# Five extra matmuls per recurrence step, and one PSUM bank for the pre-activation instead of two

## The reference, cut to what matters

```
def step(carry, tgt):
    s, c, alpha = carry
    f = lax.conv_general_dilated(alpha, conv_w, (1,), 'SAME', dimension_numbers=('NCH', 'OIH', 'NCH'))
    e = jnp.einsum('a,bta->bt', va, jnp.tanh(enc_proj + (s @ Wa_s.T)[:, None, :] + jnp.einsum('bft,af->bta', f, Wa_f) + ba))
    e = jnp.where(mask, e, jnp.float32(-1e+30))
    alpha_new = jax.nn.softmax(e, axis=1)[:, None, :]
    g = jnp.einsum('bt,btd->bd', alpha_new[:, 0], hbatch)
    y = jnp.tanh(g @ L_gy_w.T + L_gy_b + s @ L_sy.T) @ L_yy_w.T + L_yy_b
    rec = tgt @ L_ys.T + s @ L_ss.T + g @ L_gs_w.T + L_gs_b
    ig, fg, cg, og = jnp.split(rec, 4, axis=1)
    c_next = _sig(fg) * c + _sig(ig) * jnp.tanh(cg)
    s_next = _sig(og) * jnp.tanh(c_next)
    return ((s_next, c_next, alpha_new), y)
```

## Time and profile before

| what | before |
|---|---|
| median of 3 runs (lowest to highest) | 1775.03 us (1773.21 to 1776.44) |
| span of the profiled execution | 1777.0 us |
| instructions | 43152 |
| TensorE busy | 1506.0 us (85%) |
| VectorE busy | 919.2 us (52%) |
| ScalarE busy | 528.9 us (30%) |
| GpSimd busy | 387.5 us (22%) |
| granted TensorE clock, mean | 0.633 |

### The profile page before, as it was taken

One profiled execution on the slowest core, in us unless ns is written; L12 is line 12 of the kernel. 1 busy time (PEld: TensorE's weight loads), 2 busy tenths in 40 slices (PEclk: granted clock), 3 DMA queues, 4 the chain that ended last, 5 costly groups with the idle time before them and its releaser, 6 DMA issues.

```text
span 1777.0 us, 43152 instructions
## 1 busy us (share of the span) xinstructions
PE 1506.0 (85%) x15683; PEld 1022.2 (58%) x15683; DVE 919.2 (52%) x4293; ACT 528.9 (30%) x2023; POOL 387.5 (22%) x1030
## 2 busy tenths in 40 slices
PE   6547999999888888888888888888888888887999
PEld 3334454544666666666666666666666666664443
DVE  4996643331555555555555555555555555553422
ACT  1342231221333333333333333333333333331211
POOL 3344321220000222222222222222222222222211
PEclk7658999999555555555555555555555555555999
DMA  8330000001200000000000000000000000000000
GB/s 326 141 115 11 1 1 0 1 1 52 77 0 0 0 0 0 0 0 0 0 0 0 0 0 0 0 0 0 0 0 0 0 0 0 0 0 1 1 24 25
DMA packets 17363, 34.51 MB, mean 19 GB/s; under 512 B 7476, under 2 KB 8675, under 8 KB 17332
## 3 DMA queue, kind: packets, MB, share of 16 engines
q1 hardware_dynamic: 17332, 34.10, 5.3%
HBM read 32.00 MB, written 2.10 MB: 19 GB/s over the span
## 4 chain that ended last, share of the span: by engine, by line
PE 62%; DVE 25%; issue 6%; ACT 5%; POOL 1%; DVEq 1%; SPq 1%; DMA 0%; POOLq 0%; ACTq 0%
PE bank L1243 18%; PE bank L1073 11%; PE bank L1193 6%; PE bank L1088 6%; PE bank L1221 5%; ACT eh L960 4%; DVE interT L746 4%; PE bank L1199 4%; DVE krep L764 3%; PE bank L1213 3%; DVE rinv L755 3%; DVE rs L743 2%; DVE g L760 2%; PE bank L1231 2%; DVE gat L771 2%
## 5 line engine op out<-in xcount | busy, mean ns | idle before, releaser
L1243 PE MATMUL bank<-krep,uh 128*128 128x128 f32 x1024 | 313.1, 461 | 23.6
L1243 PEld LDWEIGHTS bank<-krep,uh 128*128 128x128 f32 x1024 | 237.4, 320 | 92.4 <-DVE krep L764 92.4
L493 POOL TENSOR_TENSOR sscale<-ex,rinv 128x8 f32 x256 | 51.3, 200 | 667.6 <-DVE rinv L755 667.6
L1221 PE MATMUL bank<-eh,krep 128*128 128x4 f16 x2048 | 95.3, 168 | 92.5 <-ACT eh L960 92.5
L764 DVE TENSOR_TENSOR krep<-inv,ahn 128x128 f32<-128x128 f32 x512 | 162.2, 356 | 0.0
L1073 PE MATMUL bank<-xT,wbig 128*128 128x512 f16 x672 | 157.2, 386 | 3.7 <-DVE xT L591 3.7
L743 DVE TENSOR_TENSOR rs<-bank,rin 128x8 f32<-128x8 f32 x256 | 42.8, 167 | 198.1 <-PE bank L1199 198.1
L1221 PEld LDWEIGHTS bank<-eh,krep 128*128 128x128 f16 x2048 | 74.1, 105 | 114.0 <-ACT eh L960 114.0
L963 ACT ACTIVATE xs<-gat 64x8 f32<-64x8 f32 x256 | 53.4, 208 | 288.7 <-DVE gat L771 288.7
L955 ACT ACTIVATE interT<-bank 128x128 f16<-128x128 f32 x256 | 71.2, 278 | 216.9 <-PE bank L1193 216.9
L1181 PE MATMUL bank<-enc,identb 128*128 128x128 bf16 x771 | 128.4, 303 | 0.0
(11 more groups left out here) (201 smaller groups left out, 3044.5 us busy)
## 6 DMA issues: line engine op xcount, KB each, us to landing
wbig<-d_gate_qT SPq DMA_DIRECT2D x4, 896.0 KB, 10.1
wbig<-d_up_qT SPq DMA_DIRECT2D x4, 896.0 KB, 20.7
wbig<-d_down_qT SPq DMA_DIRECT2D x1, 3584.0 KB, 30.5
d_out<-x_sb SPq DMA_DIRECT2D x8, 256.0 KB, 2.0
sscale<-d_gate_sT SPq DMA_DIRECT2D x2, 896.0 KB, 8.6
interT<-d_gate_sT SPq DMA_DIRECT2D x2, 896.0 KB, 14.9
sscale<-d_up_sT SPq DMA_DIRECT2D x2, 896.0 KB, 4.2
interT<-d_up_sT SPq DMA_DIRECT2D x2, 896.0 KB, 4.3
```

The source lines that it names most:

```text
L1221: ins = mm(bank[4][:, 4 * gp:4 * gp + 4], hg2[:, j, h, gp * P:(gp + 1) * P], e[:, 4 * h:4 * h + 4], start=(first and gp == 0 and j == 0 an ...
L1243: mm(bank[1 - par][:, 0:P], uh[:, h, :], qv[:, h, :, :], start=False, stop=False, skip_group_check=True)
```

## The change

The pre-activation of every step stands in `bank[0]`, for TensorE and for ScalarE. `bank[1]`, which is free with that, takes the results of a new helper `keep_busy(n)`: one matmul of `n` columns with the bfloat16 identity as the stationary operand and constants of the recurrence (`hg2`, float16, 128 rows) as the moving one. Nothing reads `bank[1]`. It waits for nothing but its turn on TensorE and releases nothing. There are five such calls in a step:

```
                def keep_busy(n):
                    mm(bank[1][:, 0:n], identb[:], hg2[:, 0].rearrange("p h g -> p (h g)")[:, 0:n], start=True, stop=True)
...
                    last.then_inc(s["sp_done"], 1)

+                    keep_busy(256)
                     pe.wait_ge(s["th_s"], l + 1)
...
                    for j in range(2):
                        mm(bank[3][:, 0:8], th_hi, vae2[:, j, :], start=False, stop=False, skip_group_check=True)
+                    keep_busy(256)
                    pe.wait_ge(s["th_lo_ready"], l + 1)
                    mm(bank[3][:, 0:8], th_lo, vae2[:, 0, :], start=False, stop=True, skip_group_check=True).then_inc(s["et_done"], 1)

+                    keep_busy(256)
                    pe.wait_ge(s["eh_ready"], l + 1)
...
                    masks()
-                    context_part(1 - par)
+                    context_part()
+                    keep_busy(256)

                    for h in range(2):
                        pe.wait_ge(s[f"q{h}_ready"], l + 1)
-                        mm(bank[1 - par][:, 0:P], uh[:, h, :], qv[:, h, :, :], start=False, stop=False, skip_group_check=True)
+                        mm(bank[0][:, 0:P], uh[:, h, :], qv[:, h, :, :], start=False, stop=False, skip_group_check=True)
+                    keep_busy(512)
```

More of the change, by code:

```diff
@@ L954, in _ @@
                     act.wait_ge(s["pre_done"], l + 1)
-                    nc.scalar.activation(th_hi, bank[par][:, 0:P], ACT.Tanh).then_inc(s["th_s"], 1)
-                    nc.scalar.activation(th, bank[par][:, 0:P], ACT.Tanh).then_inc(s["th_full"], 1)
+                    nc.scalar.activation(th_hi, bank[0][:, 0:P], ACT.Tanh).then_inc(s["th_s"], 1)
+                    nc.scalar.activation(th, bank[0][:, 0:P], ACT.Tanh).then_inc(s["th_full"], 1)
                     act.wait_ge(s["et_done"], l + 1)
@@ L1176, in masks, with context_part @@
                 mm(bank[3][:, 0:8], etl[:], etr[:], start=True, stop=False, skip_group_check=True)
-            def context_part(par):
+            def context_part():
                 for j in range(3):
-                    mm(bank[par][:, 0:P], identb[:], enc3[:, j, :], start=(j == 0), stop=False, skip_group_check=True)
+                    mm(bank[0][:, 0:P], identb[:], enc3[:, j, :], start=(j == 0), stop=False, skip_group_check=True)
+            def keep_busy(n):
+                mm(bank[1][:, 0:n], identb[:], hg2[:, 0].rearrange("p h g -> p (h g)")[:, 0:n], start=True, stop=True)
             masks()
-            context_part(0)
+            context_part()
             with pe.Fori(0, S // 2) as i:
@@ L1192, in _ @@
                         pe.wait_ge(s["sl_ready" if st is sl else "sh_ready"], l + 1)
-                        last = mm(bank[par][:, 0:P], was2[:, j, :], st[:].unsqueeze(2).broadcast_to([J, B, TH]),
+                        last = mm(bank[0][:, 0:P], was2[:, j, :], st[:].unsqueeze(2).broadcast_to([J, B, TH]),
                                   start=False, stop=(st is sl), skip_group_check=True)
```

## The result

| | before | after |
|---|---|---|
| median | 1774.78 us (1773.21 to 1776.44, 4 runs) | 1911.6 us (1907.34 to 1918.32, 4 runs) |
| ratio to before | | 1.0768, 95% interval 1.0736 to 1.0799 |
| span of the profiled execution | 1777.0 us | 1909.3 us |
| granted clock, mean | 0.633 | 0.628 |
| TensorE busy | 1506.0 us (85%) | 1776.4 us (93%) |

The change makes the kernel **136.8 us slower**. The forecast was 1845 us, 70 slower, with 1744 to 1865 as the range: the direction is right, the size is half of what came.

What follows compares the result with a forecast made beforehand. A chain that goes round each step of 4.52 us at the low clock, not an engine, was taken as the bound. 256 x 0.32 = +82, cut to +70 for occasional high clock: 1775 + 70 = 1845 us, range 1744 to 1865.

Steps and rivals of the forecast that it cites:

- What bounds the kernel now ... L1243 is not late: Ahead of L1193: its other supplier `sl` comes at the same moment, so a twice as fast L1243 would gain nothing.
- The call of 512 ... 0.32 us late: Between L1243 and L1193, low clock: the call makes L1193's matmul on `sl` and the chain behind it 0.32 us late.
- a hole in TensorE's columns of only 0.14 us: Between L1243's last columns (1001.76) and L1193 (1001.90): idle column time that hides part of the call of 512.
- Four calls of 256 ... Cost nothing, at either clock: Ahead of L1206, L1213, L1221 and L1243: each call's 0.21 us fits in its hole of 0.29, 0.26, 0.56 or 0.27.
- I expect that the clock rises now and then, for about one step in nine: In the 256 steps: the high clock in one of nine cuts +82 us, for all steps at the low clock, to +70.
- The direction: Whole kernel: slower than before, given a chance of 0.75.
- seem to count for little: The clock's rule: matmuls of half the rows (64 and 65) hardly help to raise the clock; no size given.
- The rival of the Trainium skill's page, that filled gaps bring the high clock: In the loop: filled gaps bring the clock to 1.00, 256 x -0.12, 1744 us; chance of the clock holding there 0.2.
- What the high clock gives: In a step: the matmul on `sl`, L1213 and L1231 get shorter, 0.12 us a step in sum.
- With 256 steps less the two thirds of one: Step length before the change: 1157.11 us of loop over 255.7 steps, 4.52 us a step.
- The range: Whole kernel: 1744 to 1865 us; the forecast's own part 1825 to 1865, stretched down to the high-clock rival's 1744.
- the tight one: The second call of 256, ahead of L1213: fits by 0.05 us alone, and costs up to 0.05 if its cover is gone.

Runs made afterwards that it cites:

- run 7: The changed kernel with more columns in its five places, 256, 512, 1024, 768 and 512, all of 128 rows (3072 a step): 1755.02 us, ratio 0.9883.
- run 8: As run 7, the same 3072 extra columns in the same places, but with 64 active rows instead of 128: 2256.46 us, ratio 1.2714.
- run 3: The changed kernel with only its matmul of 512 columns, without the calls of 256: 1883.16 us, ratio 1.0619.
- run 6: The changed kernel with its first matmul of 256 columns on 64 active rows instead of 128: 1887.12 us, ratio 1.0627.
- run 4: The changed kernel with only its first call, 256 columns ahead of the wait for th_hi: 1788.76 us, ratio 1.0082.
- run 2: The changed kernel without its matmul of 512 columns: 1798.76 us, ratio 1.0143.
- runs 5 and 11: The changed kernel with only 256 columns ahead of th_lo, 1775.2 us; and with 256 ahead of th_lo, 512 of eh, 256 of q0, 1775.11 us.
- run 10: The changed kernel with 2 x 512 instead of 256 columns ahead of the wait for eh, 2304 extra a step: 1967.95 us, ratio 1.1098.
- run 12: As run 7, without the 256 columns ahead of the wait for q0, 2816 extra a step: 1795.54 us, ratio 1.0119.

## Why the prediction was wrong in size

- *"What bounds the kernel now ... L1243 is not late"*: right in its use, that a faster L1243 gives nothing back: run 7 gains in L1197's last matmul. But it rested on the state's parts coming at the same moment; that L1193's first load stood 0.12 behind `sh`, where other waits end 0.05 behind their supplier, was the sign that the time behind L1243's last column held it, and I passed over it.
- *"The call of 512 ... 0.32 us late"*: **this step failed.** It counted "a hole in TensorE's columns of only 0.14 us" as free. That time stands between the last column with 128 rows and the first load for 64, whatever the matmul (0.11 to 0.14 behind L1243 as behind the call), moves with it, and goes when the rows are equal (run 8). The call costs its full 0.43 (run 3: 0.42). 256 x 0.10 = 26 us.
- *"Four calls of 256 ... Cost nothing, at either clock"*: **failed for the first and for the pair.** The first has two changes of the active array around it, 0.09 and 0.11, that the count of columns does not contain (run 6), and it delays an input of `eh` that has its own slack of 0.11 (run 4: 14 us). With the second, 24 us (run 2). The other two and the second alone are free (runs 5 and 11).
- *"I expect that the clock rises now and then, for about one step in nine"*: it never rose. The 82 us that I had for the low clock throughout were cut to 70 for nothing.
- *The direction* holds, and so does the low clock as the likeliest case. Its reason is not settled: matmuls of half the rows "seem to count for little" was read from two stretches; run 8 against run 7 agrees with it, but its steps are longer too, so it stays an inference. The rival of the Trainium skill's page, that filled gaps bring the high clock, holds for run 7 and not for the change; the page ("TensorE: Matmul & The Clock Gate", section "Why this matters for your kernels") warns of idle gaps, and run 10 has TensorE busy for 899.86 of 900 us at 0.50. What fills the gaps matters.
- *What the high clock gives*, 0.12 a step, was 0.10: the last matmul of L1197 takes 0.23 in run 7, not the 0.21 of the one step that I had; why they differ no run shows. L1213's share is 0.01, as taken.
- *"With 256 steps less the two thirds of one"*: that is 255.3, not 255.7, and a step of 4.53 us instead of 4.52; nothing hangs on it.
- *The range*: with the step's own bounds, 0.43 for the call of 512 and 0.05 for the tight one, the sum is 1775 + 256 x 0.48 = 1898. The range stopped at 1865, since it was drawn around the value taken; it did not contain the prediction's own upper bound for the call of 512. Even 1898 would have missed by 14.

In sum: 0.42 + 0.095 = 0.52 a step, 132 us, against 132.3 between the two profiled spans and 136.8 between the medians.

That the direction came out right rests on the call of 512, which was forecast as late and was.

## What to carry to other kernels

Work put into an engine's waits is free only if it ends before the wait does, at the speed that holds while it runs; here 1024 columns that fitted at the low clock were free (1775 us), but gave nothing either; 2304, of which many did not fit, were a loss (1968 us); and 3072, with which the clock rose, won (1755 us). Before counting a gap ahead of a wait as free, compare the distance from supplier to waiter with the same distance elsewhere in the trace (0.12 against 0.05 here): what is more than that need not be idle. Here a matmul with other active rows or columns than its neighbours brought a hold of about 0.1 us at each end; giving the filler the neighbours' rows won back 24 us (run 6). And follow every input of the instruction behind the wait, not only the latest.

## What the runs showed of the hardware that I had not expected

- At 0.50 a load of weights for a matmul with other active rows or columns started only 0.09 to 0.14 us behind the last column: 128 rows to 4, 128 to 64, 64 to 128, 6 to 128, 128 columns to 32 and 32 to 128. Between 4 rows and 6 there was no such hold, and with equal rows and columns the load came ahead of the last column (L1219 behind a call of 256 at 1004.57, with the call's columns until about 1004.69), though L1219 waits for a semaphore.
- With 3072 extra columns a step, 128 active rows gave the clock 1.00 in nearly all of the loop and 64 rows 0.50 in all of it, with steps of 4.42 and 6.39 us.
- In run 12 the two levels alternate for the whole loop, and with a mean of 0.89 it is slower than a steady 0.50 without the calls.
